# The warp's coordinate sums on GpSimd from the third group on, early weight loads postponed, and new orders of work

## The chip, the cores and the metric

One core of a Trainium2 chip. The metric is the device time of one execution in microseconds. Engines: PE is TensorE, DVE VectorE, ACT ScalarE, POOL GpSimd, SP the SyncE queue that issues most DMAs; "q" behind a name is the engine's sequencer.

## The reference, cut to what matters

128 images of 64 x 256 (8192 tokens of width 256) go through four blocks, each added to its input.

```python
x = x + ffn0(rigid_transform(x, dx, angle))      # bilinear sampling with rotation; ternary weights, 8-bit activations
x = x + moe(masked_attention_pool(x, kind))      # 4 experts of 256-1024-256, the best 2 of each token
x = x + spectral(layer_norm(x + adapter(x, language)))   # the real part of ifft(fft(x) @ w) is one 256x256 product
x = x + gated_ffn(x @ W[category] + b[category]) # ternary weights, 8-bit activations, silu gate
```

The rigid transform samples each output pixel at xp = c*gx - s*gy + dx and the like, from four neighbours, with weights that are linear in the distance.

## The kernel before, in words

The 128 images are worked in 32 groups q of four images (256 tokens). Each group passes these threads; each thread is a Python generator whose `yield`s cut it into steps, and every engine has a long string of letters in `ORDER`, written out, that says which thread takes the next step. Letters: w warp, c coords, f front (the first block's network), a attend (attention and routing), p plan, e experts, b back (adapter and spectral block), l and t last (the fourth block; t is its twin on other buffers, for the last groups), i init (ternary weights), o offsets (products of weights that are made once), h hats, g gather (on GpSimd) or geometry (on SP), s scatter, y gather of the experts' rows; on SP also r regroup, p product_weights, l rows_in and w weights_in of an expert tile, z zeros. An engine runs its string in order; a step that waits for a semaphore holds all that is behind it.

**Preparation** (`prepare`, L383 to L528). VectorE computes for every image the corner of each 4 x 8 pixel block (integer part `idx`, fraction `fr`) and the pixels' shifts inside a block (`fd`, `woff`). SP first issues the small inputs and two of five ternary matrices, then `dft` and `freq_w` (L438, L439), waits for VectorE's end (L440) and writes fd, woff, fr and idx to DRAM (L441 to L445, `s_put`, 16 each). Group 0's idx and fr are also copied in SBUF (L511, L512). SP's network part starts with a wait for `s_put` at 64 (L889).

**Warp.** GpSimd's `gather` (L1350) fetches, for each of an image's 4 blocks of a partition, a window of 33 x 4 values by an indirect DMA: 16 a group. The window buffer holds four images, so the gather of image a in group q waits for `part` of the image before it in that place (L1347), and for the landing of the second gather before it (L1349). `coords` (L910 to L920) adds fraction and shift for all pixels of a group: two adds of 128x512 (L918), x and y, into the single tile T, after `hat` has reached 2q. ScalarE's `hats` (L1423 to L1438) makes three taps of T in two halves, each after `part` shows that the half before has been used. VectorE's `warp` (L941 to L981) multiplies windows by taps, 32 products of 128x36 an image (L959), and sums them (L963, L971; L975, L976, L981 for two images together, then `part` += 2). An image is 8 w steps, a group 32. SP's `regroup` (L740) moves `W` into `C0`, with 8 DMAs an image.

**Front** on VectorE: 20 steps or so a group, among them L997 (maximum of 512 elements, from C0), L1008, L1016 (four a group, out of PSUM), L1020, L1025, which needs GpSimd's inverse root L1389, and L1111. GpSimd's front also adds a bias to the group's x (L1399, 128x512). TensorE takes 9 f steps a group (L1637, L1649, L1643, L1655). **Attend** ends with the rows of each token in the experts' sorted lists (L1105). **Plan** (L1114 to L1184) lays out tiles; its last instruction is L1178. The first plan needs groups 0 and 1. **Experts** on TensorE: `transposed` (L1746), `up` (L1761, 8 matmuls a step), `down_` (L1777, 8 a step), 82 tiles; they need the plan, the rows (L763), the weights (L769) and `i_end`, that is all five ternary matrices and the offsets (L1908, L1917, L1927, L1936 on TensorE), which read `dft`, `freq_w` and the four `moe_w2` matrices.

**SP's loads at the start:** `init` loads the third to fifth ternary matrix into two raw buffers when `i_q` says that the earlier content is used (L880, L881); `product_weights` loads the four 128x2048 matrices of `moe_w2` with no wait (L887). By shape `dft` is 128x2560 f32, `freq_w` 128x1024, each `moe_w2` part and each raw matrix 128x2048. `load_geometry` (L699) fetches a group's fr, fd and idx back from DRAM.

The step `coords` is quoted because it is what moves:

```python
            def coords(q):
                par = q % 2

                yield
                after(dve, E["hat"], 2 * q)
                dve.wait_ge(s_geo[par], 24 * (q - par) + (48 if par else 32))
                four = [[IPX, QI], [NG, PX], [1, NG]]
                for xy in range(2):
                    ins = v.tensor_tensor(ap(T, xy * QPX, four), ap(fr[par], xy * QI * NG, [[NG, QI], [0, PX], [1, NG]]),
                                          ap(fd[par], xy * QI * PX, [[PX, QI], [1, PX], [0, NG]]), ALU.add)
                ins.then_inc(E["t"], 1)
```

## Time and profile before

| | |
|---|---|
| median of 3 runs | 2107.93 us (2104.12 to 2110.24) |
| profiled execution | 2103.28 us, span 2101.5 us |
| mean granted TensorE clock | 0.955 |
| busy: TensorE, VectorE, ScalarE, GpSimd | 90%, 81%, 71%, 49% of the span |
| DMA | 369.24 MB, 176 GB/s |

The profile counts an engine as busy while an instruction runs on it; a group of rows gives busy time, the mean ns of one instruction, and the idle time before it with what ended that. Pipelined instructions overlap, so the busy time of a group can be less than count times mean. Timeline rows give start, duration, engine, line, names, shape and count, and in brackets the idle time before and its releaser.

### The profile page before, as it was taken

How to read it: one execution, taken by the hardware profiler on the slowest of the kernel's cores; microseconds unless marked ns; L12 is line 12 of the kernel's file. 1: busy time of each engine (PE TensorE's matmuls, PEld its weight loads, DVE VectorE, ACT ScalarE, POOL GpSimd, SP SyncE). 2: the span in 40 equal slices, each digit the busy share in tenths (PEclk: the TensorE clock that was granted, in tenths of full speed). 3: DMA queues.
4: the chain of work that ended last, by engine and by line, in shares of the span. 5: the costliest groups of instructions: out<-in, count | busy, mean ns of one | idle time of the engine just before them, and what ended most of it. 6: DMA issues, size and time to landing. Idle time of an engine off the chain costs nothing.

```text
span 2101.5 us, 43993 instructions
## 1 busy us (share of the span) xinstructions
PE 1881.0 (90%) x11592; PEld 1494.1 (71%) x11592; DVE 1705.9 (81%) x8017; ACT 1499.4 (71%) x2599; POOL 1025.9 (49%) x1092
## 2 busy tenths in 40 slices
PE   1652898999999999999999999999999999999876
PEld 0331686788777888887788778877777888788643
DVE  5988988999988999999999999879997445433676
ACT  3553665678868777788888887777888676574745
POOL 2655666756565565656755555545643212211230
PEclk9855999899999999999999999999999999999999
DMA  7367356764654766647665665656575546645561
GB/s 269 73 197 234 106 185 178 206 198 135 198 167 144 223 190 173 187 137 218 189 179 176 187 184 167 184 182 181 162 231 162 171 134 197 216 148 173 166 184 40
DMA packets 310642, 369.24 MB, mean 176 GB/s; under 512 B 126674, under 2 KB 257143, under 8 KB 298620
## 3 DMA queue, kind: packets, MB, share of 16 engines
q1 hardware_dynamic: 281292, 297.96, 46.5%
q0 software_dynamic: 28672, 68.21, 11.5%
q8 instruction: 96, 1.57, 0.3%
q14 instruction: 150, 1.23, 0.2%
q10 hardware_dynamic: 432, 0.27, 0.1%
HBM read 277.10 MB, written 80.79 MB: 170 GB/s over the span
## 4 chain that ended last, share of the span: by engine, by line
PE 47%; DVE 6%; SPq 4%; ACT 4%; issue 3%; POOL 2%; DMA 2%; DVEq 0%; ACTq 0%; POOLq 0%
PE bank L1761 14%; PE bank L1777 14%; PE bank L1649 5%; PE bank L1655 3%; PE bank L1852 2%; PE bank L1831 2%; PE bank L1637 2%; SPq L740 2%; PE bank L1643 1%; PE bank L1820 1%; DVE w_prod L959 1%; DMA w_win<-in_windows,w_idx 1%; POOL w_win L1350 1%; PE bank L1746 1%; PE bank L1813 1%
## 5 line engine op out<-in xcount | busy, mean ns | idle before, releaser
L1350 POOL DMA_INDIRECT w_win<-in_windows,w_idx x512 | 543.0, 1060 | 442.9 <-DMA w_win<-in_windows,w_idx 171.5
L1761 PE MATMUL bank<-moe_xT,moe_w_tile 128*128 128x256 f32 (+1 forms) x2624 | 570.2, 361 | 4.0 <-ACT moe_xT L1513 4.0
L1777 PE MATMUL bank<-moe_w,moe_hidden_T 128*128 x2336 | 570.0, 385 | 4.1 <-ACT moe_hidden_T L1530 2.0
L959 DVE TENSOR_TENSOR w_prod<-w_win,w_hat 128x36 f32<-128x36 f32 x4096 | 499.0, 217 | 18.5 <-DMA w_win<-in_windows,w_idx 9.4
L1761 PEld LDWEIGHTS bank<-moe_xT,moe_w_tile 128*128 128x128 f32 x2624 | 458.0, 192 | 67.4 <-ACT moe_xT L1513 6.1
L1777 PEld LDWEIGHTS bank<-moe_w,moe_hidden_T 128*128 128x128 f32 x2336 | 428.9, 192 | 68.6 <-issue 14.9
L1530 ACT ACTIVATE moe_hidden_T<-bank,moe_b 128x256 f32<-128x256 f32 (+1 forms) x656 | 257.7, 446 | 175.4 <-PE bank L1761 171.1
L1382 POOL DMA_INDIRECT moe_y_back<-moe_out_sorted,rows_all x128 | 130.8, 1022 | 287.6 <-DVE x_back L1209 180.1
L1368 POOL DMA_INDIRECT moe_in_sorted<-c,rows_all x128 | 143.6, 1122 | 97.7 <-issue 51.7
L1530 ACT ACT_TABLE_LOAD x99 | 127.0, 1283 | 37.1 <-PE bank L1761 34.7
L1272 DVE SCALAR_TENSOR_TENSOR hidden_back<-bank,back_stats,hidden_back 128x512 f32<-128x512 f32 x112 | 83.4, 745 | 57.1 <-ACT hidden_back L1572 56.7
L1649 PE MATMUL bank<-L_w_ternary,q1T_front 128*128 128x512 fp8e4 x256 | 82.4, 406 | 41.0 <-DVE hidden_front L1016 38.2
L1572 ACT ACT_TABLE_LOAD x90 | 115.5, 1283 | 1.9
L1016 DVE SCALAR_TENSOR_TENSOR hidden_front<-bank,front_stats,L_b_rows 128x512 f32<-128x512 f32 x128 | 95.1, 743 | 15.6 <-PE bank L1649 11.8
L1500 ACT ACTIVATE q_front<-hidden_front,half_magic,front_tile_stats 128x1024 f16<-128x1024 f32 x64 | 79.5, 1241 | 31.7 <-DVE front_tile_stats L1022 31.0
L1572 ACT ACTIVATE hidden_back<-bank,back_stats 128x512 f32<-128x512 f32 x112 | 77.0, 687 | 27.2 <-PE bank L1649 25.9
L1452 ACT ACTIVATE hidden_front<-hidden_front 128x1024 f32<-128x1024 f32 x64 | 67.8, 1060 | 28.6 <-DVE hidden_front L1016 27.8
L1197 DVE TENSOR_TENSOR moe_y<-bank,moe_offset_rows 128x512 f32<-128x512 f32 (+1 forms) x82 | 51.4, 627 | 44.4 <-PE bank L1777 36.6
L1500 ACT ACTIVATE q_back<-hidden_back,half_magic,back_tile_stats 128x1024 f16<-128x1024 f32 x56 | 69.4, 1240 | 19.4 <-DVE back_tile_stats L1279 19.2
L1504 ACT ACTIVATE q2T_front<-bank 128x1024 bf16<-128x1024 f16 x64 | 65.5, 1024 | 22.4 <-PE bank L1643 22.2
L1020 DVE TENSOR_REDUCE front_tile_stats<-hidden_front 128x1 f32<-128x1024 f32 x64 | 77.4, 1209 | 2.8 <-ACT hidden_front L1452 1.8
L1655 PE MATMUL bank<-L_w_ternary,q2T_front 128*128 128x256 fp8e4 x512 | 71.6, 286 | 7.8 <-ACT q2T_front L1504 7.8
(312 smaller groups left out, 3646.2 us busy)
## 6 DMA issues: line engine op xcount, KB each, us to landing
moe_w_tile<-in_moe_w SPq DMA_DIRECT2D x82, 1024.0 KB
L_cond_W<-in_L_cond_W SPq DMA_DIRECT2D x112, 256.0 KB
adapters<-in_adapter SPq DMA_DIRECT2D x128, 192.5 KB
moe_out_sorted<-zero_row SPq DMA_DIRECT2D x18, 1024.0 KB
gamma_beta<-in_gamma_beta SPq DMA_DIRECT2D x128, 128.0 KB
moe_x<-moe_in_sorted SPq DMA_DIRECT2D x64, 256.0 KB
moe_out_sorted<-moe_y SPq DMA_DIRECT2D x64, 256.0 KB
w_win<-in_windows,w_idx POOLq DMA_INDIRECT x512
```

Of the source, the lines that this page charges most:

```text
L959: ins = v.tensor_tensor(out3, win, hy, ALU.mult)
L1016: v.scalar_tensor_tensor(HBA[:, n * 512:(n + 1) * 512], A0[:, :], sa[:, DQ][:, one(u)], b1B[:, n * 512:(n + 1) * 512], ALU.mult, ALU.add). ...
L1350: gp.indirect_dma_start(out=V[:, g_ * WLEN:(g_ + 1) * WLEN], out_offset=None, in_=t["windows"], in_offset=bass.IndirectOffsetOnAxis(ap=idx ...
L1368: gp.indirect_dma_start(out=XS[block % 2][0:ENDROW[block] + TILE, :], out_offset=bass.IndirectOffsetOnAxis(ap=PS[:, q * 2 * TT + c:q * 2 * ...
L1382: gp.indirect_dma_start(out=YG[:, c * D:(c + 1) * D], out_offset=None, in_=YS[SUPER[q] % 2][0:ENDROW[SUPER[q]] + TILE, :], in_offset=bass. ...
L1500: return s.activation(to[:, :], hidden[:, :], ACT.Identity, bias=hmag[:, :], scale=scale)
L1530: ins = s.activation(hT[:, (f % (2 * FPU)) * TILE:(f % (2 * FPU)) * TILE + width(n)], (H0, H1)[r % 2][:, (f % FPU) * TILE:(f % FPU) * TILE ...
L1572: s.activation(L.h[:, n * 512:(n + 1) * 512], L.G[:, :], ACT.Silu, scale=L.st[:, 6 * TT + u:6 * TT + u + 1]).then_inc(L.E["b_silu"], 1)
L1649: last = te.matmul(bank[:, :], q1t[:, d * QT + u * P:d * QT + (u + 1) * P], w[:, d * F + n * 512:d * F + (n + 1) * 512], start=(d == 0), s ...
L1655: last = te.matmul(bank[:, 0:D], q2t[:, f * P:(f + 1) * P], w[:, f * D:(f + 1) * D], start=(f == 0), stop=(f == NFB - 1))
L1761: last = te.matmul((H0, H1)[r % 2][:, (f % FPU) * TILE:(f % FPU) * TILE + width(n)], W1[n % 3][:, d * F + f * P:d * F + (f + 1) * P], XT[: ...
L1777: last = te.matmul(Y[:, u * D:(u + 1) * D], hT[:, (f % (2 * FPU)) * TILE + u * P:(f % (2 * FPU)) * TILE + (u + 1) * P], ap(moe2, weight + ...
```

## The change

Four things. (1) `dft`, `freq_w`, the four `moe_w2` parts and the third to fifth ternary matrix are loaded only after `part` has reached 2, 4 or 6, that is after two, four or six images are warped; SP's thread `product_weights` has six steps in place of four. (2) The geometry is written in two parts: `fr` and `idx` first, with a semaphore of their own that is waited for before group 1's geometry, then `fd` and `woff`; the network waits for these two alone. (3) `coords` runs on VectorE for groups 0 and 1 and on GpSimd, with the same waits and shapes, for groups 2 to 31. (4) All five order strings are new; here the first 112 letters of each.

```diff
     "vector":
-        "oiciiiiwwwwcwwwwwwwwwwwwwwwwwwwwwwwiwwiwwwwwwwcwwwwwfwwfwiwiwwfwwwwowfwwwfwoowwwfwowfwiwifwwwfwwwwwcwoffwwwfawfw"
...
+        "iociiiiwwwwcwwwwwwwwwwwwwwwwwwwwwwwwwwwwwwwwwwwwwwwfwiwiwwfwwwwwfwwwwwwwfwwfiwfwiwwfwwwfwwwfwwwwwwwwffwwfwwwfwiw"
...
     "gpsimd":
-        "ggggggggggggggggggggggggggggfggggggfggggggfggggggfggggfggggggfssggssggggfggggggggssggfssgggggfgggfgggggggggggggf"
...
+        "ggggggggggggggggggggggggggcggggfgggggggfggggggfggcggfggggggggfgggfggggcgfgssggssgfgggggggfggggssggscfsgggggggfgg"
...
     "scalar":
-        "oiihhhhiiiihhioiohhiiffifhhiiffffifhhfifaafafahhfaaafffffahhaafaaaahhfffhhffffffehheaeafaehhfeeafeaffaafhehfeffe"
...
+        "ioihhhhiiiihhhhiffiihhiffihfffhfiiffohofahafifiafffahfhffaaahfahafafaafffaahhffafaafhahfefahheaeafffefhhffeeeafe"
...
     "tensor":
-        "iioooioooooiofofofofoooifffffaafafffaaafaaffffaaaaaaaaffffffffefeaeaefaefefefaeeaefaefaefaeefeefeeaefaeeafefeeaf"
...
+        "iiiffffiffofofofiofaofafofaoofofaoofaofaofaoaofafafafaafafafaffaaafafaffeaeaefefefefeafeeeeafeafefaeeeeefafeaeaf"
...
     "sync":
-        "xxggpmpppiirrggrrirgrgrrcozzzbgmrrbxzozgrrzzbzzzmxgrrtwwwglrrlogrrrrgwlmgxywlorrryrgmwlxgywlgyozzzrlrryrmxlwgyyg"
...
+        "gxgxmrrpgpigrrppirrgppigrrozzzrrgmgrrxozzzzzzzrgrcbbmgrrxbotgwwrrlwmlrrxggwlorrrrygwlmyxgwlozzzgrryrrmlwygxwlylg"
...
```

Counted in the whole strings: VectorE's first plan step stands behind 123 w, 28 f, 18 a and 5 c steps before, and behind 140 w, 40 f, 18 a and 2 c after. The last offsets step on VectorE stands behind 72 w before and 114 w after. TensorE's first e step stands behind 26 f and 16 a before, and behind 31 f and 21 a after. SP's first rows_in stands behind 14 regroup steps before and 18 after. At VectorE's w number 192 both strings have 41 a, 65 f, 1 e and 1 p behind them. On GpSimd the 30 c steps stand behind 26, 45, 62, 80, 90, 106, 122, ... 494 g steps.

```diff
@@ -376,7 +377,8 @@
         s_raw = [sem(f"p_raw{i}") for i in range(2)]
         s_ld = sem("p_ld")
         s_late = sem("p_late")
-        s_put = sem("p_geometry_out")
+        s_put = sem("p_shift_out")
+        s_rest = sem("p_index_out")
         network(nc, t, out, locals())
 
 
@@ -435,14 +437,13 @@
             sp.dma_start(pick[0:5, :], t["offset_picks"]).then_inc(s_ld, 16)
             n += 64
             assert n == NLD
-            sp.dma_start(dft[:, :], t["dft"]).then_inc(s_late, 16)
-            sp.dma_start(wf[:, :], t["freq_w"]).then_inc(s_late, 16)
             sp.wait_ge(s_pos, 2)
+            sp.dma_start(frD, fr[:, :]).then_inc(s_rest, 16)
+            sp.dma_start(idxD, idx[:, :]).then_inc(s_rest, 16)
+            sp.wait_ge(s_pos, 3)
             sp.dma_start(fdD.rearrange("(c b x) -> b c x", c=2, b=B),
                          fd[:, :].rearrange("p (c x) -> p c x", c=2)).then_inc(s_put, 16)
             sp.dma_start(offD.rearrange("o (b x) -> (o b) x", b=B), woff[:, :]).then_inc(s_put, 16)
-            sp.dma_start(frD, fr[:, :]).then_inc(s_put, 16)
-            sp.dma_start(idxD, idx[:, :]).then_inc(s_put, 16)
 
         @block.scalar
         def _(act):
@@ -509,7 +510,7 @@
             ch.link(v.tensor_tensor(idx[:, :].rearrange("p (b g) -> p b g", b=B),
                                     ap(gfl, 0, [[NG, B], [1, NG]]), ap(wcst, W_BASE, [[1, B], [0, NG]]), ALU.add))
             v.tensor_copy(idx0[:, :], idx[:, 0:QI * NG])
-            v.tensor_copy(ap(fr0, 0, [[QI * NG, 2], [1, QI * NG]]), ap(fr, 0, [[B * NG, 2], [1, QI * NG]]))
+            v.tensor_copy(ap(fr0, 0, [[QI * NG, 2], [1, QI * NG]]), ap(fr, 0, [[B * NG, 2], [1, QI * NG]])).then_inc(s_pos, 1)
             cols = lambda tile, n: ap(tile, 0, [[n, 2], [1, n]])
             step_of = lambda off, n: ap(step, off, [[1, 2], [0, n]])
             v.tensor_scalar(sM, sA, float(GI - 1), 0.0, ALU.mult, ALU.min)
@@ -702,6 +703,8 @@
                     sp.wait_ge(E["t"], q - 1)
                     for a in range(2 * QI):
                         sp.wait_ge(s_win[a], 8 * NG * (q - 1))
+                if q == 1:
+                    sp.wait_ge(s_rest, 32)
                 if q:
                     sp.dma_start(fr[par][:, :].rearrange("p (c g) -> p c g", c=2),
                                  frD.rearrange("p (c g) -> p c g", c=2)[:, :, bass.ds(q * QI * NG, QI * NG)]).then_inc(s_geo[par], 16)
@@ -878,15 +881,22 @@
                 for i in range(2, len(BITW)):
                     yield
                     sp.wait_ge(E["i_q"], i - 1)
+                    sp.wait_ge(E["part"], 2 * (i - 1))
                     sp.dma_start(raw[i % 2][:, :], t[BITW[i]]).then_inc(s_raw[i % 2], 16)
 
-            def product_weights(e):
-
-                yield
-                cols = slice(e * NFB * D, (e + 1) * NFB * D)
-                sp.dma_start(moe2[:, cols], t["moe_w2"][:, cols]).then_inc(s_late, 16)
-
-            sp.wait_ge(s_put, 64)
+            def product_weights(n):
+
+                yield
+                sp.wait_ge(E["part"], 2 * (n // 2 + 1))
+                if n == 0:
+                    sp.dma_start(dft[:, :], t["dft"]).then_inc(s_late, 16)
+                elif n == 1:
+                    sp.dma_start(wf[:, :], t["freq_w"]).then_inc(s_late, 16)
+                else:
+                    cols = slice((n - 2) * NFB * D, (n - 1) * NFB * D)
+                    sp.dma_start(moe2[:, cols], t["moe_w2"][:, cols]).then_inc(s_late, 16)
+
+            sp.wait_ge(s_put, 32)
             load_geometry(0, 0)
             load_offsets(0, 0)
             sp.wait_ge(s_ld, NLD)
@@ -897,7 +907,7 @@
                   tails=each(tails, range(NSB)), list_in=each(rows_in, range(GT)),
                   weights=each(weights_in, range(GT)), y_out=each(moe_out, range(GT)), back=each(back_in, q_),
                   cond=each(last_in, ONES), qcond=each(last_in, TWINS), store=each(store, ONES), vstore=each(store, TWINS), init=each(init, range(1)),
-                  product_weights=each(product_weights, range(EXP)))
+                  product_weights=each(product_weights, range(2 + EXP)))
             for k in range(4):
                 sp.wait_ge(s_out[k], 16 * sum(home(q) == k for q in q_))
 
@@ -1327,12 +1337,24 @@
             q_ = range(NQ)
             weave("vector", front=each(dense(ch, front, 2), q_), attend=each(dense(ch, attend, 2), q_), back=each(back, q_),
                   last=each(last, ONES), twin=each(last, TWINS), plan=each(dense(ch, make_plan, 1), range(NBK)), experts=each(evict, range(GT)),
-                  warp=each(warp, q_), coords=each(coords, q_), init=each(init, range(1)), offsets=each(offsets, range(1)))
+                  warp=each(warp, q_), coords=each(coords, range(2)), init=each(init, range(1)), offsets=each(offsets, range(1)))
 
 
         @block.gpsimd
         def _(pool):
             pc = Chain(pool, E["pool_steps"])
+
+            def coords(q):
+                par = q % 2
+
+                yield
+                after(pool, E["hat"], 2 * q)
+                pool.wait_ge(s_geo[par], 24 * (q - par) + (48 if par else 32))
+                four = [[IPX, QI], [NG, PX], [1, NG]]
+                for xy in range(2):
+                    ins = gp.tensor_tensor(ap(T, xy * QPX, four), ap(fr[par], xy * QI * NG, [[NG, QI], [0, PX], [1, NG]]),
+                                          ap(fd[par], xy * QI * PX, [[PX, QI], [1, PX], [0, NG]]), ALU.add)
+                ins.then_inc(E["t"], 1)
 
             def gather(q):
                 par = q % 2
@@ -1413,7 +1435,7 @@
 
             q_ = range(NQ)
             weave("gpsimd", front=each(front, q_), y_back=each(y_back, q_), back=each(back, q_), scatter=each(scatter, q_),
-                  gather=each(gather, q_))
+                  gather=each(gather, q_), coords=each(coords, range(2, NQ)))
 
 
         @block.scalar
```

Left out: the two places where the new semaphore `s_rest` is handed on by name.

## Rows read from the trace of the kernel before

**Rows 1.** The page: span, busy time by engine, and the chain by engine.

```profile
span 2101.5 us, 43993 instructions
PE 1881.0 (90%) x11592; PEld 1494.1 (71%) x11592; DVE 1705.9 (81%) x8017; ACT 1499.4 (71%) x2599; POOL 1025.9 (49%) x1092
...
PE 47%; DVE 6%; SPq 4%; ACT 4%; issue 3%; POOL 2%; DMA 2%; DVEq 0%; ACTq 0%; POOLq 0%
```

**Rows 2.** Windows: stretch, length, busy us per engine, granted clock, DMA share, GB/s.

```profile
25.00:50.00 25.00, 3.18 (x9) 2.71 (x10) 10.54 (x68) 15.85 (x16) 11.12 (x9) 1.00 0.84 300
150.00:200.00 50.00, 15.13 (x50) 8.18 (x50) 41.50 (x241) 17.39 (x34) 29.65 (x30) 0.50 0.77 243
200.00:250.00 50.00, 36.43 (x190) 28.34 (x191) 45.32 (x241) 28.98 (x54) 28.67 (x30) 0.82 0.40 117
209.82:236.08 26.26, 21.28 (x110) 16.41 (x109) 25.21 (x127) 17.81 (x37) 17.36 (x17) 0.90 0.32 72
250.00:300.00 50.00, 47.55 (x268) 40.11 (x267) 45.49 (x269) 34.22 (x69) 33.87 (x38) 1.00 0.50 145
250.00:1600.00 1350.00, 1301.69 (x8095) 1064.51 (x8094) 1233.28 (x6240) 1059.25 (x1896) 795.43 (x843) 0.98 0.61 180
```

**Rows 3.** Waits of TensorE from 100 to 250, then TensorE's and VectorE's from 250 to 1600.

```profile
PE bank L1649 <- DVE hidden_front L1016: 23.8, 8, 12.3
...
PE bank L1649 <- DVE hidden_front L1016: 9.9, 7, 4.4
...
DVE front_tile_stats L1025 <- POOL front_tile_stats L1389: 22.3, 15, 4.5
```

**Rows 4.** Timeline: start, us, engine, line. First plan, first expert step, L1721.

```profile
190.85 0.18 DVE L1178 TENSOR_TENSOR plan<-plan_work,const 128x21 int32<-128x21 f32 x1
...
209.82 1.06 PE L1746 MATMUL bank<-const,moe_x 128*128 128x128 f32 x4
...
236.08 0.61 PE L1721 MATMUL bank<-x_router,xT_front 128*128 128x4 f32 x4 [0.75 <-ACT xT_front L1482]
```

**Rows 5.** Timeline of the start, all engines.

```profile
29.90 0.95 POOL L1350 DMA_INDIRECT w_win<-in_windows,w_idx  x1 [2.55 <-DMA w_win<-in_windows,w_idx]
...
30.20 0.33 SPq L887 DMA_DIRECT2D moe_w<-in_moe_w  x1
30.43 1.29 DVE L918 TENSOR_TENSOR w_t<-w_frac,w_shift_frac 128x512 f32<-128x512 f32 x2 [5.08 <-DMA w_shift_frac<-w_shift_frac_all]
...
33.46 0.63 ACT L1438 ACTIVATE w_hat<-w_t 128x512 f32<-128x512 f32 x1
...
39.35 3.74 DVE L959 TENSOR_TENSOR w_prod<-w_win,w_hat 128x36 f32<-128x36 f32 x32 [6.25 <-DMA w_win<-in_windows,w_idx]
...
47.60 3.72 DVE L959 TENSOR_TENSOR w_prod<-w_win,w_hat 128x36 f32<-128x36 f32 x32 [2.27 <-DMA w_win<-in_windows,w_idx]
```

**Rows 6.** Groups: L1761, L1016 of the whole span, L1917 from 40 to 100.

```profile
L1761 PE MATMUL bank<-moe_xT,moe_w_tile 128*128 128x256 f32 (+1 forms) x2624 | 570.2, 361 | 4.0 <-ACT moe_xT L1513 4.0
...
L1016 DVE SCALAR_TENSOR_TENSOR hidden_front<-bank,front_stats,L_b_rows 128x512 f32<-128x512 f32 x128 | 95.1, 743 | 15.6 <-PE bank L1649 11.8 <-issue 1.8 <-ACT q_front L1500 1.2
...
L1917 PE MATMUL bank<-moe_w,gelu_b_columns 128*5 128x256 f32 x64 | 17.0, 423 | 0.0
```

**Rows 7.** Groups, one line's min/median/max in ns, and GpSimd beside VectorE in the timeline.

```profile
L918 DVE TENSOR_TENSOR w_t<-w_frac,w_shift_frac 128x512 f32<-128x512 f32 x64 | 41.1, 683 | 5.2 <-DMA w_shift_frac<-w_shift_frac_all 5.1
...
L1008 DVE SCALAR_TENSOR_TENSOR front_stats<-front_stats,weight_means x32: 180/208/1265, 82.0 to 1637.6; 128x2 f32<-128x2 f32 x32
...
115.38 1.38 POOL L1399 TENSOR_TENSOR x_front<-x_front,L_b_rows 128x512 f32<-128x512 f32 x1
...
115.55 3.82 DVE L959 TENSOR_TENSOR w_prod<-w_win,w_hat 128x36 f32<-128x36 f32 x24
...
443.01 1.27 POOL L1399 TENSOR_TENSOR x_front<-x_front,L_b_rows 128x512 f32<-128x512 f32 x1
...
443.18 0.67 DVE L997 TENSOR_REDUCE front_stats<-c 128x2 f32<-128x512 f32 x1
```

155 lines of the change are left out of this document (78 added, 77 removed).

## The prediction

> **What bounds the kernel now.** The page first: TensorE is busy 90% of the 2101.5 us and holds 47% of the chain that ended last; VectorE is busy 81% and holds 6% of it [rows 1]. An average over stages with different limits decides nothing, so the windows view comes next [rows 2]. From 250 to 1600 us TensorE is busy 1301.7 of 1350 us and VectorE 1233.3: TensorE bounds, VectorE is close behind. Before 250 us it is otherwise: from 150 to 200 us TensorE does 15.1 us of work, at a granted clock of 0.50 (the 1.2 GHz level), while VectorE is busy 41.5 of 50. So the start belongs to VectorE, which warps the first groups, and it ends when the experts' tiles give TensorE something to fill itself with. The waits say the same: from 100 to 250 us TensorE waits 23.8 us for L1016 on VectorE alone, and in the 1350 us after it only 9.9 us for the same line, with VectorE itself waiting 22.3 us there for GpSimd's L1389 [rows 3].
>
> What ends the start is read in the timeline [rows 4]: the first plan is written at 190.85 us, and TensorE's first expert step stands at 209.82. From there on each microsecond that TensorE idles is lost, and little else counts.
>
> **The change, part by part.**
>
> *Weight loads postponed, geometry written earlier.* Four matrices of 1 MB, the DFT and frequency matrices, and three of the five ternary matrices now wait for images of group 0. In the trace the fourth window gather of image 0 is issued at 29.90 us, among the loads of L887, the first at 30.20. VectorE waits 5.08 us for the shift fractions (30.43) and 6.25 us for that gather (39.35), then 2.27 us for the second image (47.60) [rows 5]; the DMA engines are at 0.84 of their time and 300 GB/s between 25 and 50 us [rows 2]. Without the loads the hats decide. Two geometry writes are waited for in place of four, and the queue is emptier: I take 3 of the 5.08 us off. The first half of the hats ends at 34.09 (33.46 + 0.63), so it moves to 31, and the first product with it, from 39.35. That is 8.3 us, and with the 2.27 us up to 10.6. But the six moved loads, 6.0 MB by their shapes, are still to come, and they now land on the gathers of group 1, while VectorE has two images ready. At 300 GB/s they take 20 us, beside the raw matrices. I give back 3 us (bounds: 0, and the old waits again, 6.25 + 2.27 = 8.5). VectorE is ahead by 7.5 us (2 to 10.6).
>
> *What of it reaches the experts.* The orders count here. In VectorE's new order the first plan stands behind 140 warp steps and 40 front steps, before behind 123 and 28; three coordinate pairs fewer stand ahead. An image takes from 39.35 to 47.60 less the wait of 2.27 and a coordinate pair of 1.29: 4.7 us for its 8 warp steps, 0.6 each [rows 5]. A front step is taken at 0.5 (the commonest large one, L1016, is 0.743 [rows 6]). So 17 x 0.6 + 12 x 0.5 - 3 x 1.29 = 12.3 us more before the plan, less 7.5 us: the plan at 196, the first expert step 5 us later than 209.82. Against it, TensorE has done more by then: its new order has 31 front and 21 attend steps ahead of the first expert step, before 26 and 16. The old run reached that twenty-first attend step (L1721) at 236.08 [rows 4]; of the 26.3 us since 209.82 TensorE was busy 21.3 [rows 2]. Nine expert steps were in it, two of them transposes of some 1 us, seven of 8 matmuls at 570.2/2624 us each [rows 6], 14 in all, at part of the lower clock more. So the steps now done ahead are worth 5 to 7 us. These two cancel. What stays is that fronts are ahead afterwards: TensorE idled 13.6 us from 200 to 250 and 2.5 from 250 to 300 [rows 2], mostly for VectorE. I take 5 of these 16 (0 to 12). **Start: -5 us.**
>
> *The offsets' matmuls* (L1917, 17.0 us, the largest [rows 6], L1908, L1927) move from an idle stretch to between the first fronts. The cover is TensorE's idle share from 100 to 200 us, two thirds. If the clock is at its lower level there they take up to twice as long, and each can hold a front step by 4 us: 0, with +6 as the bad end.
>
> *Coordinates on GpSimd.* 60 of the 64 L918 instructions, 683 ns each but 1.29 us for a pair in the pipeline, leave VectorE: 30 x 1.29 = 38.7 us. On GpSimd the nearest row is L1399, an add of the same 128x512: 1.38 and 1.27 us [rows 7]. So 60 x 1.32 = 79 us go to an engine that is busy 795 of 1350 us in the middle; no row shows the coordinates' short inner runs there, so twice that is the upper bound. It does not come free to VectorE. L1008, which follows GpSimd's roots and so often meets L1399, takes 208 ns in the median and up to 1265. Beside the L1399 at 115.38, 24 products took 3.82 us, where 32 took 3.74 at 39.35 [rows 5], 2.8 for 24. Beside the one at 443.01 a reduction (L997) took 0.67, no more than L918's 683 ns for as many elements [rows 7]. Two of the three cases were held, by 1.06 and 1.02 us. The products and sums of the warp have two SBUF operands like the held ones, and the coordinates will run in their midst. I take 0.9 us an instruction: 54 us of holds against 38.7 saved, so VectorE is **worse off by 15 us**. Bounds: no hold, -38.7; held for the whole of each, 79 - 38.7 = +40.
>
> The Trainium skill has a rule that speaks against this move (page "SBUF — State Buffer", section "SBUF: two separate sides"): a VectorE instruction with two SBUF inputs, or in a two-port mode, and a GpSimd instruction exclude each other for the whole of whichever came first. By that rule alone the move would stand at the bound of +40 us on VectorE, where the three cases average 0.69 us a hold and give +3. The trace agrees with the rule in what is held and what is not, the reduction included.
>
> How much of the 15 us reaches the end: VectorE has 1350 - 1233 = 117 us idle in the middle, and TensorE idles 48 us there, of which 9.9 are for L1016 [rows 2, 3]; I take 28 as VectorE's part, midway. In proportion 15/117 of 28 us: **+3.6 us** (-9 to +20; the far end where the holds fall on what TensorE waits for). GpSimd's queue: a pair of 2.6 us stands in front of gathers, scatters and the inverse roots, for which VectorE already waits 22.3 us [rows 3]; it also waits for the hats of the group before, with the gathers behind it. The orders put it behind a gather that waits for the same image, so this is +1 (0 to +5).
>
> *New order* otherwise: from the 192nd warp step on the counts of front, attend, plan and expert steps on VectorE are the same within one or two, so 0, with 5 us either way for the luck of an order.
>
> **Sum** on the profiled execution: 2103.3 - 5 + 3.6 + 1 = 2102.9, a change of -0.4 us. That execution lies 4.6 us below the median of the runs, 2107.93; the prediction for the median is 2107.5.
>
> **Rivals.** *Lockout decides (slower).* The place is the middle, 250 to 1600 us: holds fall on the products, the group's interval grows, TensorE waits at L1649 for L1016. For it: VectorE is busy 91% there, and the cases shown lost 1.0 us each. Against: 117 us of idle time. If VectorE loses 24 to 40 us net and half passes, that is +12 to +20, less the start's 5: about 2119. It decides once VectorE's busy share in the middle is above 94%. The Trainium skill's rule, above, is this case at its end. *The start is kept whole (faster).* The loads collide with nothing, the plan is not later than before, and TensorE's fill begins 5 us earlier with 8 us of the idle 16 gone; holds no larger than the saving. -13 and 0: about 2095. For it: gathers are spread over a group; against: the plan stands behind 17 more warp steps. *The postponement only moves the wait.* The loads then stop group 1's gathers as they stopped group 0's: the 8.5 us come back, the start gives 0 to +3 and the sum is about 2113, still inside what can't be told. A quarter of the middle case. It could also be that the first wait was not due to these loads, since other small loads stand at 25 to 30 us; the price is the same.
>
> **How the numbers follow.** A measurement of this kernel can tell 0.3%, 6.3 us, from no change: faster is below 2101.6, slower above 2114.3. The forecast with the moved wait holds 0.40; the kept start, with those ends of the other terms that help, 0.31; the lockout, with the offsets' bad end, 0.29. The bounds of single terms would reach from -30 to +45, but not together: the range goes from 2090 (start kept, some relief) to 2125 (a lockout past its middle), leaving 0.1 on either side. The middle case's own range is 2101.6 to 2114.3.
>
> **What would show it.** Right: the first product near 31 us; a wait for windows of a few microseconds between 55 and 75; the plan later than 190.85 in spite of it; L918's successor on GpSimd near 1.3 us; VectorE's busy time in the middle up in spite of 60 instructions fewer, the products' mean above 217 ns; TensorE's waits there for L1016 a little above 9.9. Wrong: a first expert step well ahead of 210 us, VectorE's busy time down by 30 us or more, or coordinates on GpSimd that take over 2 us each.

## The result, and the profile after

| | before | after |
|---|---|---|
| median (range) | 2107.66 us (2104.12 to 2110.24) | 2149.64 us (2146.27 to 2155.94) |
| ratio | | 1.0218 (1.0193 to 1.0242) |
| profiled execution, its span | 2103.3, 2101.5 | 2155.94, 2153.9 |

The change costs 42 us by the medians (the ratio, taken over the runs of both kernels, has an interval from 1.9 to 2.4%). The forecast was no change, 2107.5, with a range up to 2125. The profiled execution of the changed kernel is the longest of its four, 6 us above the median, so its rows show 52 us of loss and not 42. Its page, which answers to [rows 1]:

```profile
PE 1876.7 (87%) x11592; PEld 1495.9 (69%) x11592; DVE 1737.1 (81%) x7957; ACT 1515.3 (70%) x2610; POOL 1085.4 (50%) x1152
```

TensorE has the same 11592 matmuls and even 4 us less busy time; the loss is its idle time. VectorE executes 60 instructions fewer and is busy 31 us longer. The windows (stretch, length, busy us and instructions of TensorE, its weight loads, VectorE, ScalarE and GpSimd, granted clock, DMA share, GB/s), first of the kernel before and then of the changed one:

```profile
0.00:250.00 250.00, 116.17 (x498) 73.33 (x499) 200.99 (x1055) 121.80 (x186) 129.44 (x135) 0.73 0.58 177
250.00:600.00 350.00, 327.46 (x1959) 270.96 (x1958) 317.00 (x1721) 249.29 (x484) 223.08 (x232) 0.96 0.60 178
600.00:1000.00 400.00, 392.89 (x2438) 326.76 (x2437) 368.74 (x1922) 314.65 (x577) 241.78 (x257) 1.00 0.62 184
1000.00:1300.00 300.00, 293.39 (x1852) 237.50 (x1852) 281.75 (x1368) 253.56 (x427) 175.50 (x192) 1.00 0.61 179
```

```profile
0.00:250.00 250.00, 94.69 (x424) 57.93 (x425) 196.34 (x1014) 115.87 (x175) 138.46 (x142) 0.83 0.56 172
250.00:600.00 350.00, 322.84 (x1917) 269.80 (x1916) 316.05 (x1662) 235.60 (x466) 221.54 (x236) 0.97 0.58 176
600.00:1000.00 400.00, 378.50 (x2326) 314.34 (x2325) 367.25 (x1878) 302.28 (x557) 259.31 (x271) 0.99 0.58 172
1000.00:1300.00 300.00, 286.12 (x1774) 229.03 (x1774) 281.92 (x1326) 244.77 (x407) 187.20 (x197) 1.00 0.61 181
```

The number in brackets behind TensorE's time, its matmuls, serves as a rough clock of progress: rough, because another order also brings other matmuls first. Added up, the changed kernel is 74 matmuls behind at 250 us, 116 at 600, 228 at 1000, 306 at 1300. At the rate of the middle (1852 in 300 us, 6.2 a microsecond) that is 12, 19, 37 and 49 us: a quarter of the loss falls in the start, the rest in the middle. The 49 us fit the 52 of the two profiled executions.

What TensorE waits for from 250 to 1600 us, and VectorE (engine, line, who releases it: total us, times, longest), beside [rows 3]:

```profile
PE bank L1671 <- DVE hidden_front L1026: 16.6, 13, 3.9
PE bank L1665 <- DVE x_front L1121: 13.4, 6, 3.0
PE bank L1799 <- DVE moe_y L1207: 10.7, 8, 2.8
...
DVE front_tile_stats L1035 <- POOL front_tile_stats L1411: 36.7, 18, 4.9
```

All three of TensorE's are waits for something that VectorE hands over (9.9, 6.4 and 1.4 us before). No one wait holds the loss. The start, in the timeline (L969 is the warp's product, L1121 the front's output, L1188 the plan, L1659 a transpose of front or attend, L1768 the first of an expert tile; the 16 products at 73.23 are the part of 32 that the window held):

```profile
32.25 3.74 DVE L969 TENSOR_TENSOR w_prod<-w_win,w_hat 128x36 f32<-128x36 f32 x32 [2.44 <-DMA w_win<-in_windows,w_idx]
...
64.49 3.71 DVE L969 TENSOR_TENSOR w_prod<-w_win,w_hat 128x36 f32<-128x36 f32 x32 [6.11 <-DMA w_win<-in_windows,w_idx]
...
73.23 1.89 DVE L969 TENSOR_TENSOR w_prod<-w_win,w_hat 128x36 f32<-128x36 f32 x16 [3.77 <-DMA w_win<-in_windows,w_idx]
...
109.31 6.18 DVE L969 TENSOR_TENSOR w_prod<-w_win,w_hat 128x36 f32<-128x36 f32 x32
...
119.06 0.47 DVE L1121 SCALAR_TENSOR_TENSOR x_front<-bank,front_tile_stats,x_front 128x256 f32<-128x256 f32 x1
...
121.63 1.06 PE L1659 MATMUL bank<-const,x_front 128*128 128x128 f32 x4
...
209.21 0.17 DVE L1188 TENSOR_TENSOR plan<-plan_work,const 128x21 int32<-128x21 f32 x1
...
231.86 1.09 PE L1768 MATMUL bank<-const,moe_x 128*128 128x128 f32 x4 [4.78 <-DMA moe_x<-moe_in_sorted]
```

The first product is 7 us earlier than in [rows 5], but the waits for windows come back one group later (6.11 and 3.77 against 6.25 and 2.27). The first plan is 18 us later and the first expert step 22 us later than in [rows 4].

What the postponed loads do is plain when the end of each group's warp is set beside a run with the same order and early loads (`e3`, below). Groups 0 and 1, first in the changed kernel, then in `e3`:

```profile
57.77 0.61 DVE L991 TENSOR_TENSOR w_out<-w_cols 128x256 f32<-128x256 f32 x1
...
97.91 0.61 DVE L991 TENSOR_TENSOR w_out<-w_cols 128x256 f32<-128x256 f32 x1
```

```profile
67.57 0.61 DVE L989 TENSOR_TENSOR w_out<-w_cols 128x256 f32<-128x256 f32 x1
...
99.13 0.61 DVE L989 TENSOR_TENSOR w_out<-w_cols 128x256 f32<-128x256 f32 x1
```

Group 0 is done 9.8 us earlier, group 1 only 1.2 us. The traffic moved with it: the DMA engines are busy 0.33 of 25 to 50 us and 0.88 of 50 to 75 in the changed kernel, 0.92 and 0.39 in `e3`.

And the coordinates on GpSimd, beside VectorE:

```profile
242.31 3.06 DVE L969 TENSOR_TENSOR w_prod<-w_win,w_hat 128x36 f32<-128x36 f32 x8
...
242.48 2.05 POOL L1355 TENSOR_TENSOR w_t<-w_frac,w_shift_frac 128x512 f32<-128x512 f32 x2
...
153.73 7.13 DVE L969 TENSOR_TENSOR w_prod<-w_win,w_hat 128x36 f32<-128x36 f32 x32
...
154.19 2.06 POOL L1355 TENSOR_TENSOR w_t<-w_frac,w_shift_frac 128x512 f32<-128x512 f32 x2
...
159.49 1.30 POOL L1421 TENSOR_TENSOR x_front<-x_front,L_b_rows 128x512 f32<-128x512 f32 x1 [0.24 <-DMA x_front<-in_x]
```

Eight products of usually 0.97 us took 3.06, that is 2.09 more, beside a pair of 2.05. Thirty-two, usually 3.7, took 7.13 beside a pair and the bias add: 3.4 more, which is 2.06 + 1.30. In these two cases VectorE does not get in between the two adds of a pair. It can, though: one pair of this trace took 2.33 us, and L986 ran between its adds, with L1176 held before it and L1178 behind it.

```profile
769.65 2.33 POOL L1355 TENSOR_TENSOR w_t<-w_frac,w_shift_frac 128x512 f32<-128x512 f32 x2
...
769.79 0.95 DVE L1176 TENSOR_TENSOR plan_work<-plan_work,const 128x8 f32<-128x8 f32 x1
770.66 0.41 DVE L986 TENSOR_TENSOR w_cols<-w_cols 128x256 f32<-128x256 f32 x1
771.00 1.00 DVE L1178 TENSOR_TENSOR tiles_begun<-tiles_begun,plan_work 128x4 f32<-128x4 f32 x1
```

The longest of all 4096 products tells the same without picking cases (ns: shortest, median, longest). In the kernel before it is longer by about one add, in the changed one by more than a pair, and in the last run below (`p2c`), where GpSimd makes no large add from the bias, hardly at all:

```profile
L959 DVE TENSOR_TENSOR w_prod<-w_win,w_hat x4096: 184/214/1346, 39.3 to 1585.1; 128x36 f32<-128x36 f32 x196
```

```profile
L969 DVE TENSOR_TENSOR w_prod<-w_win,w_hat x4096: 181/212/2818, 32.2 to 1643.3; 128x36 f32<-128x36 f32 x196
```

```profile
L959 DVE TENSOR_TENSOR w_prod<-w_win,w_hat x4096: 180/216/317, 39.2 to 1580.4; 128x36 f32<-128x36 f32 x196
```

### The profile page after: what moved, and what is told of

Same layout as the page of the kernel before. It is cut to its first block and busy times, and to the rows that moved or that the text cites. A ratio compares the mean times of both kernels' runs of the same rounds, so it can differ in the third digit from the quotient of the medians.

```text
span 2153.9 us, 44015 instructions
## 1 busy us (share of the span) xinstructions
PE 1876.7 (87%) x11592; PEld 1495.9 (69%) x11592; DVE 1737.1 (81%) x7957; ACT 1515.3 (70%) x2610; POOL 1085.4 (50%) x1152
## 5 line engine op out<-in xcount | busy, mean ns | idle before, releaser
L1783 PE MATMUL bank<-moe_xT,moe_w_tile 128*128 128x256 f32 (+1 forms) x2624 | 577.1, 364 | 0.3 <-ACT moe_xT L1535 0.2
L969 DVE TENSOR_TENSOR w_prod<-w_win,w_hat 128x36 f32<-128x36 f32 x4096 | 529.5, 224 | 19.6 <-DMA w_win<-in_windows,w_idx 13.0
L1390 POOL DMA_INDIRECT moe_in_sorted<-c,rows_all x128 | 137.9, 1077 | 103.5 <-issue 70.0
L1456 ACT ACTIVATE w_hat<-w_t 128x512 f32<-128x512 f32 x64 | 40.4, 632 | 66.0 <-DVE w_out L991 64.2
L1207 DVE TENSOR_TENSOR moe_y<-bank,moe_offset_rows 128x512 f32<-128x512 f32 (+1 forms) x82 | 51.4, 626 | 39.5 <-PE bank L1799 32.0
L1522 ACT ACTIVATE q_back<-hidden_back,half_magic,back_tile_stats 128x1024 f16<-128x1024 f32 x56 | 69.6, 1243 | 15.3 <-DVE back_tile_stats L1289 13.7
```

Source lines behind the costliest of these rows:

```text
L969: ins = v.tensor_tensor(out3, win, hy, ALU.mult)
L1390: gp.indirect_dma_start(out=XS[block % 2][0:ENDROW[block] + TILE, :], out_offset=bass.IndirectOffsetOnAxis(ap=PS[:, q * 2 * TT + c:q * 2 * ...
L1522: return s.activation(to[:, :], hidden[:, :], ACT.Identity, bias=hmag[:, :], scale=scale)
L1783: last = te.matmul((H0, H1)[r % 2][:, (f % FPU) * TILE:(f % FPU) * TILE + width(n)], W1[n % 3][:, d * F + f * P:d * F + (f + 1) * P], XT[: ...
```

## The experiments

A *hold*, below, is time for which a VectorE instruction stands still beside a GpSimd add. Two theories at the outset. **L**: GpSimd's pair holds VectorE, and VectorE passes that on to TensorE. **O**: the new order and the postponed loads cost it. All ratios are to the kernel before on the same chip, with their 95% intervals; us behind a ratio are worked out from it. The diffs leave out the order strings where they are long.

### The parts one by one

Old order, coordinates on GpSimd (`e1_old_order_coords_gpsimd`), each `c` at the place in GpSimd's string where VectorE ran it in time:

```diff
-  coords=each(coords, q_), init=...                 # vector
+  coords=each(coords, range(2)), init=...
-  gather=each(gather, q_))                          # gpsimd
+  gather=each(gather, q_), coords=each(coords, range(2, NQ)))
```

> The kernel before, its loads and its order, with one thing changed: the coordinate pairs from the third group on run on GpSimd, each at the place in GpSimd's order where VectorE ran it in time. Theory L (the pair of adds on GpSimd locks VectorE out for 2.05 us, where 1.29 are saved, and VectorE, 91% busy in the middle, hands that on): VectorE's busy time up by 20 to 31 us, TensorE's idle time from 250 to 1600 us up by 15 to 30, start unchanged, so 2125 to 2140 us. Theory O (the new order and the postponed loads cost it all): TensorE's idle time unchanged, 2106 to 2113 us.

New order, coordinates back on VectorE (`e2_new_order_coords_vector`), the same lines the other way:

> The changed kernel, its loads and its order, with the coordinate pairs back on VectorE, each at the place where GpSimd ran it in time. Theory L: the middle's 28 us of extra idle time of TensorE go, the start's 22 and the end's 12 stay: 2120 to 2130 us. Theory O: 2143 to 2152 us. If both parts add up, this run's gain over the changed kernel equals the loss of the run with the old order and coordinates on GpSimd.

New order, loads early (`e3_new_order_early_loads`), and the same with the coordinates on VectorE, the new order alone (`e4_new_order_alone`):

```diff
-  sp.wait_ge(E["part"], 2 * (i - 1))                # init
-  sp.wait_ge(E["part"], 2 * (n // 2 + 1))           # product_weights
-  "sync": "gxgxmrrpgpigrrppirrgppig..."
+  "sync": "gxgxpmpppppiirrggrrrrgig..."
```

> The changed kernel with the loads' waits for the images of group 0 taken out and the loads put back in front of the gathers on SyncE's queue; order of all else and coordinates on GpSimd as changed. If the postponed loads make the start late (theory O, its first half): plan(0) back near 200 us, 2135 to 2143 us. If the order alone does: the first product goes back to about 39 us, VectorE is 4 to 8 us later at the plan, and the time is 2149 to 2156 us.

> The changed kernel with both edits taken back, the coordinates on VectorE and the loads early: what is left is the new order (and the split of the geometry writes). Theory O, order half: 2128 to 2140 us, with the plan at 205 us or later. Theory L alone: 2108 to 2115 us, since nothing but the coordinates would cost anything.

And the zero of the last one, the old order in the changed code with coordinates on VectorE and early loads (`f1_old_order_split`):

> The old order in the code of the changed kernel, coordinates on VectorE and loads early: of the change only the split of the geometry writes is left. Every theory: within 3 us of the kernel before, 2105 to 2111 us. It is the zero for the next run.

Measured. VectorE's busy time, plan, expert step and matmuls are those of the profiled execution (for the second row the longest of its ten, 9 us above the median). Matmuls are counted by 250 and by 1600 us, from the windows; plan and expert step are the first ones:

| order | coordinates | loads | ratio | VectorE busy | plan, expert step | matmuls by 250, 1600 |
|---|---|---|---|---|---|---|
| old | VectorE | early | 1 (before) | 1705.9 | 191, 210 | 498, 8593 |
| old, split | VectorE | early | 1.0013 (0.9999 to 1.0027) | 1703.5 | 195, 215 | 474, 8526 |
| old | GpSimd | early | 1.0067 (1.0036 to 1.0097) | 1731.0 | 193, 212 | 483, 8471 |
| new | VectorE | early | 1.0095 (1.0062 to 1.0127) | 1717.9 | 204, 226 | 466, 8500 |
| new | VectorE | late | 1.0116 (1.0088 to 1.0144) | 1715.7 | 205, 228 | 447, 8436 |
| new | GpSimd | early | 1.0244 (1.0207 to 1.0280) | 1740.9 | 211, 234 | 414, 8303 |
| new | GpSimd | late (the change) | 1.0218 (1.0193 to 1.0242) | 1737.1 | 209, 232 | 424, 8279 |

Three readings. The order alone costs 0.8 to 1% (17 to 20 us). The coordinates cost 0.67% (14 us) in the old order and 1.0 to 1.5% (21 to 31 us) in the new one. Postponing the loads shows nothing: +0.2% with the coordinates on VectorE, -0.3% with them on GpSimd, inside the intervals. So both theories hold a half. Together the halves cost more than their sum: 2.4% against 1.6 with early loads, clear of the intervals, and 2.2% against 1.8 with late ones, not clear of them.

### Where the new order loses

Old order up to the end of the sixth group's warp, new order for all the rest (`f2_old_start_new_rest`), on the code of `f1` (the strings are written out in the kernel; this says in short how they are made):

```diff
-  ORDER[e] = new[e]
+  ORDER[e] = old[e][:cut] + (new[e] without the steps already taken)
```

> As the run above, with the old order up to the end of the warp of the sixth group (192 warp steps on VectorE, about 265 us) and the new order for all that is left. New order alone cost 17 us. Theory S (the start: the new order brings the first plan and the first expert step some 18 us later): the loss is gone, 2106 to 2113 us, and the first expert step stands near 210 us. Theory M (the new order is worse in the middle and at the end): the loss stays, 2119 to 2126 us.

Measured: 1.0168 (1.0146 to 1.0190), plan 189, first expert step 208. The start is restored and the kernel is slower than with the new order throughout: above what either theory had, and no sign that the start holds the loss. The splice has a seam of its own, so the windows decide. Windows of the new order alone, then of this splice:

```profile
0.00:250.00 250.00, 105.12 (x466) 64.60 (x466) 200.45 (x1068) 121.05 (x183) 132.32 (x137) 0.83 0.56 172
250.00:600.00 350.00, 329.26 (x2002) 275.45 (x2002) 317.94 (x1710) 247.38 (x484) 219.18 (x231) 0.98 0.60 181
600.00:1000.00 400.00, 386.07 (x2371) 319.99 (x2369) 375.46 (x1973) 315.85 (x577) 241.70 (x258) 1.00 0.61 183
```

```profile
0.00:250.00 250.00, 111.71 (x494) 70.28 (x494) 203.55 (x1080) 124.43 (x191) 125.97 (x138) 0.74 0.59 180
250.00:600.00 350.00, 316.68 (x1888) 262.92 (x1889) 305.40 (x1654) 234.37 (x460) 212.89 (x223) 0.95 0.57 172
600.00:1000.00 400.00, 383.70 (x2345) 317.15 (x2344) 369.31 (x1927) 310.47 (x564) 239.07 (x254) 0.99 0.60 176
```

The new order alone is 32 matmuls behind at 250 us and 11 ahead at 600 (466 + 2002 against 498 + 1959): its late plan is made good. It loses 67 matmuls, 11 us, from 600 to 1000, and is 93 behind at 1600, 15 us of the 16 by which its profiled execution is longer. The splice starts level and loses 71 from 250 to 600, where the two orders join, and 93 more from 600 to 1000. So theory S, that the start holds the loss, fell.

What TensorE waits for from 250 to 1600 us in the new order alone (`e4`):

```profile
PE bank L1796 <- DVE moe_y L1204: 7.1, 5, 3.3
PE bank L1656 <- DVE c_adapter L1247: 6.5, 6, 2.2
PE bank L1668 <- DVE hidden_back L1279: 5.2, 7, 1.4
```

In the kernel before these three were 1.4, 2.7 and 0.9 us, while the wait for the front's L1023 (L1016 before) went only from 9.9 to 12.2. With the new strings TensorE stands at the experts and the back before VectorE has served them. Which steps of the strings do it is not shown.

The inversion of two steps in the start (`g1_attend_before_next_front`): the changed kernel, with the first attend steps of groups 0 and 1 ahead of the next group's first front steps.

```diff
-  "scalar": "ioihhhhiiiihhhhiffiihhiffihfffhfiiffohofahafifiafffahfhffaaahfahaf...
+  "scalar": "ioihhhhiiiihhhhiffiihhiffihfffhfiifafohofhafifiafffahfhfafaaahfhafafa...
-  "tensor": "iiiffffiffofofofiofaofafofaoofofaoofaofaofaoaofafafafaa...
+  "tensor": "iiiffffiffofofofioafofafofaoofofaoofaofaofaoaoaffafafaafafa...
```

> The changed kernel as it is, with the first attend step of groups 0 and 1 put ahead of the first front step of the next group on TensorE and on ScalarE, as the old order has it (four steps moved). In the changed kernel the transposes of group 0 wait 6.6 us, those of group 1 4.6 us behind a front step whose input is not there. Theory S1 (this inversion makes the start late): group 1's transposes at 162 instead of 167 us, the plan 5 to 12 us earlier than 209, 2138 to 2146 us. Theory S2 (VectorE's order decides: the second half of the front's output stands behind a whole image): the plan at most 3 us earlier, 2146 to 2152 us.

Measured: 1.0245 (1.0206 to 1.0284), plan 213 in place of 209. Group 0's transposes came 3.6 us earlier (118.00 instead of 121.63) and the plan did not; group 1's came 3.6 us later (170.93 instead of 167.34). So theory S1 fell, and the plan was not even the 3 us earlier that S2 allows. Which steps of the new order cost the 17 us stays open; no run exchanged the string of one engine alone.

### What a pair on GpSimd costs

Each pair done twice (`h1_gpsimd_pair_twice`), on `e1`:

```diff
   for xy in range(2): ins = gp.tensor_tensor(...)
+  pc.link(ins)                                      # the second pair waits for the first
+  for xy in range(2): ins = gp.tensor_tensor(...)
   ins.then_inc(E["t"], 1)
```

> The old order with the coordinate pairs on GpSimd, each pair done twice (the same sums written again): nothing is taken off VectorE for the second pair, so this is the price of a pair that locks it out. Theory L, at 2.05 us a pair: VectorE's busy time up by another 50 to 62 us over the run with one pair, its products' mean from 225 to 235 ns or more, and the time up by 20 to 45 us, to 2142 to 2167. If a pair held VectorE for only the 0.9 us an instruction of the prediction or less, beside the reductions and gathers: up by 30 us or less. If not the hold but GpSimd's queue set the cost, VectorE's busy time would stay and its waits for GpSimd's roots would grow instead.

Measured: 1.0323 (1.0304 to 1.0343), VectorE busy 1770.5 us (39.5 over `e1`), products at a mean of 231 ns. The second pair adds 1.3 us to VectorE's busy time, less than the first, yet costs 2.6%, 54 us: more time than VectorE is held. The hats can start 2.1 us later in each group, but that is hardly felt: ScalarE waited for the coordinates 6.0 us in all here, in two places, and 1.6 us in `e1`, and VectorE's products waited for windows 8.1 us here and 8.0 in `e1`. What makes up the rest of the 54 us is not shown.

The other end: no coordinates after the second group (`n1_coords_left_out`, VectorE sums one element in their place), and one element on GpSimd (`n2_one_element_on_gpsimd`). Both make the images from the third group on from old coordinates.

```diff
-  for xy in range(2): ins = gp.tensor_tensor(...)
+  ins = gp.tensor_tensor(ap(T, 0, [[1, 1]]), ap(fr[par], 0, [[1, 1]]), ap(fd[par], 0, [[1, 1]]), ALU.add)
```

> The kernel before, in which the coordinate pairs from the third group on are left out: VectorE writes one element in their place, so the later hats are made from old coordinates and the images warped from them are not the reference's. It is the best that the move could bring: 30 pairs of 1.29 us, 38.7 us, off VectorE and no hold at all. Prediction's way of passing VectorE's time on (15 of 117 us idle, times 28): 9 us, 2091 to 2099 us beside a before of 2100 to 2107. If VectorE's order passes on most of it, as the run with the pairs twice suggests: 20 to 35 us faster.

> The old order with the coordinates' places on GpSimd, but one element summed there in place of the two adds of 128x512 (the rest of the coordinates from the third group on is left out, the images are not the reference's). It has the move's waits and its place in GpSimd's queue, without its 2.05 us of hold. If the hold is the whole price (theory L): as fast as the run with the coordinates left out, within 3 us. If the place in the queue costs (theory Q: the hats wait for GpSimd): half or more of the distance to the run with the real adds on GpSimd is left.

These were run, with two kernels of the next section, on a chip where the kernel before itself took 2303.23 us, at a granted clock of 0.92 to 0.93, with VectorE busy 1037 us of the middle 1350 in `n1` (1204 in `n2c`, below, at the usual speed). Ratios 1.0077 (1.0037 to 1.0118) and 1.0125 (1.0084 to 1.0165): with less work on VectorE both are slower. Beside a kernel before of 2284.09 us none was faster either: `n1b` 1.0109 (1.0024 to 1.0194), `n2b` 1.0043 (0.9997 to 1.0090), and the changed kernel with one element on GpSimd, `o1_new_order_one_element`, 1.0054 (1.0013 to 1.0094).

> The kernel before with the coordinate pairs from the third group on left out (one element in their place on VectorE; later images are not the reference's), again, on a chip where the kernel before takes about 2105 us. 38.7 us come off VectorE. By the prediction's way of passing time on: 9 us faster. By the passing seen where time was added (25 us added gave 14, 40 gave 36 to 54): 20 to 35 us faster.

> The old order with the coordinates' places on GpSimd and one element summed in each (the rest left out, as above). Hold alone (theory L): within 4 us of the run with the coordinates left out, and VectorE's products at a mean of 217 to 218 ns. Queue and hats (theory Q): 10 us or more above it.

> The changed kernel, with one element summed on GpSimd in place of the two adds (later coordinates left out, later images not the reference's). Theory L: all that the hold cost goes, and the 38.7 us of VectorE's own pairs do not come back: below the new order with coordinates on VectorE, so 2095 to 2118 us. Theory Q: 2125 to 2140 us.

At that speed neither theory can be read: the chain that ended last in `n1` holds 8% "another core or an unknown queue" (none in the kernel before), and what does that was not found. Beside a kernel before at the usual speed, 2110.86 us:

> The old order with the coordinates' places on GpSimd and one element summed in each (the rest left out), a third time, hoped for a chip where the kernel before takes about 2105 us. Theory L: at least as fast as the kernel before, 0 to 30 us faster, where the real adds made it 14 slower. Theory Q: 7 us slower or more.

Measured: 0.9972 (0.9949 to 0.9994), 5.9 us faster, VectorE busy 1675.1 us. The waits and the place in GpSimd's queue thus cost less than the 31 us off VectorE bring, and theory Q fell as far as the waits go (the pair's own 2.05 us in the queue are not in this run). From `e1`'s +0.67% to these -0.28% it is 20 us, the price of the two adds themselves, with the caution that the two runs are from two chips. The products of `n2c` and of `e1`:

```profile
L960 DVE TENSOR_TENSOR w_prod<-w_win,w_hat 128x36 f32<-128x36 f32 x4096 | 498.4, 218 | 15.7 <-DMA w_win<-in_windows,w_idx 8.4 <-issue 5.3 <-ACT w_hat L1449 1.1
```

```profile
L960 DVE TENSOR_TENSOR w_prod<-w_win,w_hat 128x36 f32<-128x36 f32 x4096 | 530.6, 225 | 17.9 <-issue 8.0 <-DMA w_win<-in_windows,w_idx 8.0 <-ACT w_hat L1451 1.1
...
L1346 POOL TENSOR_TENSOR w_t<-w_frac,w_shift_frac 128x512 f32<-128x512 f32 x60 | 61.7, 1053 | 1.3 <-ACT w_hat L1451 0.6
```

### The other way round

GpSimd's bias adds of front (`p1_front_add_on_vector`) and of front and back (`p2_both_adds_on_vector`) taken to VectorE, ahead of its waits for GpSimd's roots; the kernel before otherwise:

```diff
-  gp.tensor_tensor(tile3(XA[par][:, :]), ..., ap(b2B, ...), ALU.add).then_inc(E["a_xb"], 1)     # GpSimd, front
-  gp.tensor_tensor(tile3(X[:, :]), ..., ap(fbB, ...), ALU.add).then_inc(E["b_xf"], 1)           # GpSimd, back
+  dve.wait_ge(E["x"], 16 * (q + 1))
+  v.tensor_tensor(...).then_inc(E["a_xb"], 1)       # VectorE, front, before the wait for a_rms
+  v.tensor_tensor(...).then_inc(E["b_xf"], 1)       # VectorE, back, before the wait for b_pow
```

> The other way round: the kernel before, with the front's bias add (32 adds of 128x512, 1.32 us each on GpSimd) taken to VectorE ahead of its wait for GpSimd's root, coordinates on VectorE as before. Theory L: 32 x 0.65 = 20.7 us more on VectorE, up to 42 us of holds fewer, so VectorE's busy time down by 10 to 21 us and the time by 5 to 20. If a hold is only 0.69 us on average, as in the three cases of the prediction: nothing either way, within 4 us. If holds are rare: 5 to 15 us slower.

> As the run above, with the 32 adds of the back (x plus the frequency bias, 128x512, 1.36 us each on GpSimd) on VectorE too, ahead of its wait for GpSimd's root. Theory L: another 10 to 20 us off VectorE's busy time where these adds meet products, less late in the run, where VectorE is idle half of the time; 8 to 30 us faster than before. If the place of the add on VectorE delays the layer norm behind it: no faster than the run above.

> The kernel before with the 64 bias adds of front and back (128x512) on VectorE instead of GpSimd. Theory L: 64 x 0.65 = 42 us more work on VectorE, up to 80 us of holds fewer; on the slow chip VectorE's busy time came to 1710 where the kernel before has 1706, so the two cancel. Then 0 to 8 us faster, since the adds stand in waits of VectorE for GpSimd's roots; slower by 5 or more if VectorE's place in the order decides.

> The kernel before with the 64 bias adds of front and back on VectorE instead of GpSimd. On the two slow chips the ratio to the kernel before was 0.996 and 0.993. Theory L: 0.993 to 0.999 here too, since holds go and the adds stand where VectorE waits for a root. If only the slow chips' idle VectorE hid the adds: 1.000 to 1.006.

Measured: `p1`, only beside the 2303.23 us, 1.0019 (0.9977 to 1.0061), undecided. Both adds: 0.9964 (0.9928 to 1.0000) there, 0.9928 (0.9886 to 0.9971) beside the 2284.09 us, and at the usual speed **0.9935 (0.9913 to 0.9957): 2095.81 us, faster than both kernels**. Windows and VectorE's groups of that last run:

```profile
250.00:1600.00 1350.00, 1304.18 (x8113) 1065.70 (x8111) 1229.04 (x6276) 1062.18 (x1901) 748.66 (x796) 0.98 0.61 181
```

```profile
L959 DVE TENSOR_TENSOR w_prod<-w_win,w_hat 128x36 f32<-128x36 f32 x4096 | 490.4, 217 | 19.3 <-DMA w_win<-in_windows,w_idx 10.0 <-issue 7.3 <-ACT w_hat L1436 1.3
...
L1008 DVE TENSOR_TENSOR x_front<-x_front,L_b_rows 128x512 f32<-128x512 f32 x32 | 21.8, 680 | 1.0 <-issue 1.0
...
L1239 DVE TENSOR_TENSOR x_back<-x_back,freq_bias_rows 128x512 f32<-128x512 f32 x28 | 19.2, 684 | 0.2
```

VectorE takes on 41 us of adds in these two rows (four more of 0.69 us are in the twin's buffers) and is busy 9 us less (1696.8 against 1705.9): some 50 us of holds went with the 80 us of adds that GpSimd no longer makes. The largest part is in the back's two lines that stood beside GpSimd's add, L1234 and L1240, 34.2 and 43.4 us before and 28.0 each now; the products gave 8.6. GpSimd is busy 68 us less. VectorE's waits for GpSimd's roots hardly changed, 41.6 us in all before and 38.2 here. How the gain of 13.7 us divides between VectorE's holds and GpSimd's shorter queue is not separated.

## Why the prediction was wrong

Three steps failed: the term of 0 for the new order, which costs 17 to 20 us; the quarter by which VectorE's time was passed on, 3.6 us where 14 to 31 came; and the plan's place in the start, which gave -5. The hold on VectorE, the mechanism that the forecast took for the coordinates, was right and nearly of the right size.

**The first product: right.** 31 expected, 32.25 measured. **The give-back was mis-sized**: 3 us were taken, with the old 8.5 as the bad end, and 9.9 came. The rival "only moves the wait" describes the loads well, and they cost nothing that can be measured either way.

**"The plan at 196": failed.** VectorE was ahead by the figure that was said (the warp of group 1 ends at 98.5 instead of 105.5, 7.5 expected), but not by the loads: with the same order and early loads it ends at 99.7 (`e3`) and 98.3 (`e4`). The new order has less of other work ahead of that point, and the agreement was luck. The plan came at 209. With the order alone it is at 204. The step counted the warp and front steps ahead of the plan and priced them at their durations, 12.3 us. The plan does not hang on a count: it hangs on a chain through four engines (front's output, attend's transposes, scores, routing). That chain reached the second half of the front's output at 119.06 instead of 113.50, since an image's 32 products, held to 6.18 us, stand ahead of it, and group 0's rows at 167 instead of 147. The hold is 2.4 us of these 20; with the order alone the two stand at 115.92 and 162. The work that TensorE does ahead was to cancel the late plan; with the order alone it did, by 600 us, as the prediction had in kind, and in the changed kernel it did not (116 matmuls behind at 600).

**"From the 192nd warp step the counts are the same, so 0": failed.** The new order alone costs 17 to 20 us, and by the matmuls all of it falls after 600 us. Equal counts at one place say nothing of which step waits behind which, and 5 us either way was far too narrow for an order exchanged whole. *The offsets' matmuls* are part of that order and have no run of their own. Their largest line takes 15.9 us in the new place, from 122.6 to 148.8 us, and 17.0 in the old. Their cover was read too large: TensorE is idle 59 of the 100 us from 100 to 200, not two thirds.

**The coordinates: the mechanism right, two sizes off.** The hold was 0.9 us an instruction in the prediction, 54 us. Measured between `n2c` and `e1`: 1731.0 - 1675.1 = 55.9 us, 0.93 each. Reaching the size so closely has luck in it: it was a choice between the 0.69 us of three cases and the 1.32 of a whole add. The Trainium skill's rule (page "SBUF — State Buffer", section "SBUF: two separate sides") would have a VectorE instruction with two SBUF inputs held for the whole of each add. With the 61.7 us of the group above that is, as an estimate, at most 62 us, and this trace agrees but for a tenth. The saving was mis-sized: 38.7 us taken, 1705.9 - 1675.1 = 30.8 measured; L918's own 38.5 us went, and VectorE's other rows grew by some 8, which is not explained. Net 25 us in place of 15.

**How it passes to the end: failed.** The prediction passed VectorE's time on in proportion, 28/117, about a quarter. The runs at the usual speed, in the old order:

| | VectorE busy against before | time against before |
|---|---|---|
| one element on GpSimd | -30.8 us | -5.9 us |
| a pair on GpSimd | +25.1 | +14.1 |
| the pair twice | +64.6 | +68 |

Of time taken off a fifth comes through, near what the prediction had; of time added more than half, and then all. Each row has one more cause in it, so this is the outcome of three runs and no law: the first keeps the waits on GpSimd, which may hide a part of the gain, and the other two lengthen GpSimd's queue as well. In the new order a pair's 21 us (1737.1 - 1715.7) cost 1.0%, also 21 us, with late loads, and 23 us (1740.9 - 1717.9) cost 1.5%, 31 us, with early ones. VectorE's share in the middle stood at 91% before, 92% with a pair (1240.4 of 1350 us) and 90% in the changed kernel, so the threshold of the lockout rival (above 94%) never came. The share does not rise although VectorE is busy 31 us longer in all: in the same window it gets through fewer instructions (5990 against 6240), its work being spread over a longer time. The sign "VectorE's busy time in the middle up" therefore failed in the change (1215 against 1233 us), and came true in `e1` (1240). The mean of the products (217 to 224 ns) and the waits of TensorE did show it. "TensorE's waits for L1016 a little above 9.9" would have been right for the pair in the old order (10.1) and was 16.6 in the change (12.2 with the order alone). *GpSimd's queue*, +1 in the sum, shows in one row: in the changed kernel GpSimd sat idle 15.3 us for ScalarE's hats before its adds, in three places and with the gathers behind it; in `e1`, with the old order, 0.6 us.

```profile
L1355 POOL TENSOR_TENSOR w_t<-w_frac,w_shift_frac 128x512 f32<-128x512 f32 x60 | 62.1, 1060 | 16.1 <-ACT w_hat L1460 15.3
```

That may be a part of why the coordinates cost more in the new order; no run takes it out.

**The rival "lockout decides"** had the right place, sign and price (24 to 40 us, half passed, +12 to +20) and a chance of 0.29. It missed by the order's 17 to 20 us beside it, by its partner, the start, counted at -5, and by the 7 to 17 us by which the two do more together than apart.

## What to carry to other kernels

Price an elementwise add that moves to GpSimd by its whole duration against a VectorE full of two-operand work (0.93 of 1.05 us here). Where VectorE is 90% busy in front of a TensorE with a fixed order, let the bad end of the range have all of the added time reach the end. Then ask for the opposite move: GpSimd's remaining large adds may be dearer where they are, as here. And never cost a wholesale new order at zero by counting steps; follow the chain that reaches the first plan, and give the rest a range of a per cent or more.
